# One chunk of a conv-attention block taken slot by slot on TensorE, VectorE's conv steps moved one place up, and fc1 as 32x32 tiles

## The reference, cut to what matters

```python
# layer 0
h = biasfree_ln(x, ln1_w)
x1 = gelu(depthwise3x3(h[:, :16]))            # local branch
q, k, v, lfeat = split(gelu(conv1x1(h[:, 16:])))   # 8 channels each
attn = swapaxes(softmax(avg_pool(q) @ max_pool(k).T, axis=1))
out = concat([x1, lfeat, attn @ v]) + x
m = biasfree_ln(out, ln2_w)
m = gelu(fc1(m))                              # 32 -> 128 channels
m = m + gelu(depthwise3x3(m) + pos_b)
X = out + fc2(m)                              # 128 -> 32 channels
# layer 1, over 256 pixels of every image
q, k, v = X.T @ Wq + bq, X.T @ Wk + bk, X.T @ Wv + bv
a = softmax(q @ k.T, axis=1)                  # 256 x 256, over the queries
y = X + (a @ v).T
```

## Time and profile before

| | us |
|---|---|
| median of three runs (lowest, highest) | 119.53 (118.51, 121.95) |
| the profiled execution's own time | 119.45 |
| its span, first to last instruction | 117.7 |
| TensorE matmul busy (share of the span) | 101.3 (86%) |
| ScalarE busy | 86.7 (74%) |
| VectorE busy | 75.2 (64%) |
| TensorE in the chain that ended last | 64% |

### The profile page before, as it was taken

How to read it: one execution, slowest core, us unless ns; L and a number is a source line. 1 busy time by engine, 2 the same in 40 slices (tenths; PEclk the granted TensorE clock), 3 DMA queues, 4 the chain that set the end, 5 groups by cost and what they waited for, 6 DMA issues and landing times.

```text
span 117.7 us, 5736 instructions
## 1 busy us (share of the span) xinstructions
PE 101.3 (86%) x2632; PEld 58.4 (50%) x2632; DVE 75.2 (64%) x152; ACT 86.7 (74%) x204; POOL 12.1 (10%) x22
## 2 busy tenths in 40 slices
PE   0394999789999899998999799999799999997660
PEld 0042677566684446832445464534364566575330
DVE  0007992133332989799957698964746579789851
ACT  4069991851785883889567989947889989898960
POOL 5010000000000000000000000598000040002300
PEclk9999999995589999999999999999999999999999
DMA  2880000000000000000000000000000020002022
GB/s 61 277 336 16 0 6 6 0 6 0 6 6 6 8 0 6 8 6 0 6 0 6 0 6 6 0 0 6 6 6 0 0 95 0 6 15 77 0 89 89
DMA packets 1751, 3.42 MB, mean 29 GB/s; under 512 B 320, under 2 KB 576, under 8 KB 1728
## 3 DMA queue, kind: packets, MB, share of 16 engines
q1 hardware_dynamic: 1584, 3.03, 7.4%
q10 hardware_dynamic: 144, 0.03, 0.2%
HBM read 2.01 MB, written 1.05 MB: 26 GB/s over the span
## 4 chain that ended last, share of the span: by engine, by line
PE 64%; ACT 16%; DVE 11%; DMA 3%; issue 3%; ACTq 0%; DVEq 0%
PE ps L372 13%; PE ps L295 10%; ACT prob L749 6%; PE ps L455 6%; PE ps L420 4%; PE ps L483 4%; ACT hpad L700 4%; DVE unit L917 3%; DMA first<-first_in 3%; PE ps L284 3%; PE ps L262 3%; PE ps L467 3%; PE ps L448 3%; ACT prob L736 3%; PE ps L307 2%
## 5 line engine op out<-in xcount | busy, mean ns | idle before, releaser
L372 PE MATMUL ps<-hpad,third 32*32 32x450 f32 (+2 forms) x864 | 36.5, 563 | 0.6 <-ACT hpad L700 0.5
L749 ACT ACTIVATE prob<-ps,smax 128x256 f32<-128x256 f32 x56 | 25.7, 479 | 3.7 <-DVE smax L964 3.7
L917 DVE SCALAR_TENSOR_TENSOR unit<-hpad,third,unit 128x544 f32<-128x544 f32 x32 | 23.8, 796 | 0.0
L964 DVE TENSOR_REDUCE smax<-ps 128x2 f32<-128x512 f32 x26 | 16.5, 683 | 6.5 <-PE ps L467 3.4
L372 PEld LDWEIGHTS ps<-hpad,third 32*32 32x32 f32 x864 | 14.0, 103 | 8.9 <-issue 4.2
L295 PE MATMUL ps<-npad,second 32*32 32x225 f32 (+2 forms) x576 | 14.6, 390 | 0.3 <-DVE npad L841 0.3
L239 POOL TENSOR_TENSOR v_tok<-v_tok,row_inv 128x256 f32<-128x256 f32 x7 | 5.1, 738 | 94.0 <-DVE row_inv L974 94.0
L700 ACT ACTIVATE hpad<-ps,third 128x1024 f32<-128x1024 f32 x8 | 8.7, 1116 | 4.5 <-PE ps L356 2.4
L749 ACT ACTIVATION_READ_ACCUMULATOR prob<-ps,smax 128x1 f32 x56 | 11.8, 211 | 0.0
L295 PEld LDWEIGHTS ps<-npad,second 32*32 32x32 f32 x576 | 9.2, 107 | 3.4 <-issue 1.7
L483 PE MATMUL ps<-prob,v_tok 128*32 128x256 f32 x128 | 8.1, 382 | 2.3 <-ACT prob L736 1.1
(11 more groups left out here) (83 smaller groups left out, 140.4 us busy)
## 6 DMA issues: line engine op xcount, KB each, us to landing
x<-x_in SPq DMA_DIRECT2D x4, 256.0 KB, 5.2
y<-m SPq DMA_DIRECT2D x3, 256.0 KB, 2.5
third<-third_in SPq DMA_DIRECT2D x1, 456.5 KB, 6.5
second<-second_in SPq DMA_DIRECT2D x1, 453.5 KB, 5.4
y<-m SPq DMA_DIRECT2D x2, 128.0 KB, 1.9
first<-first_in ACTq DMA_DIRECT2D x1, 33.0 KB, 4.1
```

What stands on the lines that cost most here:

```text
L372: last = pe.matmul(inside(pixels(ps[quadrant(rotated(r, g)), banks[g], :]), tap), c3("taps")[quadrant(r), tap * C:(tap + 1) * C], inside(p ...
L749: last = act.activation(prob[:, G * (slot_turn(s) % PROBS) + g, jt * NPIX:(jt + 1) * NPIX], ps[:, banks[q], jt * NPIX:(jt + 1) * NPIX], AC ...
L917: dve.scalar_tensor_tensor(out=sums, in0=source, scalar=weight, in1=sums, op0=ALU.mult, op1=ALU.add).then_inc(unit_step, 1)
L964: dve.tensor_reduce(smax[:, s, 2 * q:2 * q + 2], ps[:, banks[q], :].rearrange("p (j i) -> p j i", j=2), AX_X, ALU.max, negate=True).then_i ...
```

## The change

TensorE: fc1 of chunks 0 and 2 goes by `fc1_by_tiles`, and `fc1` is deleted. The taps of chunk 3's convolution are spread anew: before fc2 of chunk 2 stands tap 1 of groups 0 and 1 only, and its other half comes behind it. `queries_and_keys(2)` becomes a new `query_beside_key` for slot 4 (keys into bank 6, queries into bank 7, no tap in between) and for slot 5 (banks 4 and 5, half of tap 2 in between), each with its own semaphore step. Slot 4's scores go by halves as slot 5's did: quadrants 2 and 3 as soon as slot 4's key and query are biased, then quadrants 0 and 1, with tap 3 beside both. `scores_beside_tap` is only written in another way. Two taps, 7 and 8, are now left for the place behind `fc2_units(0, 6)`, where one was; `query_and_key(0, 4)` moves ahead of `weighted_values(2, 7)`.

ScalarE: only slot 4's key stays there; slot 5's key goes to VectorE.

VectorE: one more step of the chunk-0 convolution at each of three places, so that two steps fewer are left between the last maxima of slot 3 and X of slot 4; `query(4)`, `key(5)`, `query(5)`, and maxima of slot 4 by halves. Counts of semaphores follow.

```diff
@@ -163,7 +163,7 @@
             return {1: 1 + s % 2, 2: 3 + s % 2, 0: 5, 3: 6 + s % 2}[s // 2]
 
         def slot_of_qk(s):
-            return {0: 1, 1: 2, 6: 3, 7: 4}[s]
+            return {4: 1, 5: 2, 0: 3, 1: 4, 6: 5, 7: 6}[s]
 
         def slot_turn(s):
             return 2 * turn_of(s // 2) + s % 2
@@ -345,11 +345,6 @@
                                          start=True, stop=True)
                 last.then_inc(mixed, 1)
 
-            def fc1(k, g, bank):
-
-                pe.matmul(ps[:, bank, :], c3("fc1_w")[quadrant(g), :], m[quadrant(g), k, :],
-                          start=True, stop=True).then_inc(fc1_done, 1)
-
             def fc1_by_tiles(k, g, bank):
 
                 for c in range(G):
@@ -361,7 +356,7 @@
 
                 pe.wait_ge(normed[1], k + 1)
                 for g in range(G):
-                    fc1(k, g, banks[g])
+                    fc1_by_tiles(k, g, banks[g])
 
             def conv_taps(k, lo, hi, banks, groups=range(G), rows=range(G)):
 
@@ -438,6 +433,13 @@
                 project("wk", s, bank, 0)
                 project("wq", s, bank, 1).then_inc(qk_of_slot, 1)
 
+            def query_beside_key(s, key_bank, query_bank, tap, groups):
+
+                pe.wait_ge(X_ready, x_count(s))
+                project("wk", s, key_bank)
+                conv_taps(s // 2 + 1, tap, tap + 1, LOW, groups)
+                project("wq", s, query_bank).then_inc(qk_of_slot, 1)
+
             def values(k, bank):
 
                 pe.wait_ge(X_ready, x_count(2 * k + 1))
@@ -457,19 +459,21 @@
                                          slot(rstd, s)[quadrant(q), :], start=True, stop=True)
                 last.then_inc(scores_done, 1)
 
+            def scores_by_tiles(s, jt, quadrants, banks):
+
+                for q in quadrants:
+                    for c in range(G):
+                        at = jt * P + c * C
+                        last = pe.matmul(ps[quadrant(c), banks[q], jt * NPIX:(jt + 1) * NPIX],
+                                         slot(swapped, s)[quadrant(q), at:at + C],
+                                         slot(rstd, s)[quadrant(q), :], start=True, stop=True)
+                return last
+
             def scores_beside_tap(s, quadrants, banks, tap, conv_banks):
 
-                rows = [r for r in range(G) if r not in quadrants]
-                for jt in range(2):
-                    for q in quadrants:
-                        for c in range(G):
-                            at = jt * P + c * C
-                            last = pe.matmul(ps[quadrant(c), banks[q], jt * NPIX:(jt + 1) * NPIX],
-                                             slot(swapped, s)[quadrant(q), at:at + C],
-                                             slot(rstd, s)[quadrant(q), :], start=True, stop=True)
-                    if jt == 0:
-                        conv_taps(s // 2 + 1, tap, tap + 1, conv_banks, rows=rows)
-                last.then_inc(scores_done, 1)
+                scores_by_tiles(s, 0, quadrants, banks)
+                conv_taps(s // 2 + 1, tap, tap + 1, conv_banks, rows=[r for r in range(G) if r not in quadrants])
+                scores_by_tiles(s, 1, quadrants, banks).then_inc(scores_done, 1)
 
             def weighted_values(s, bank):
 
@@ -559,7 +563,7 @@
             pe.wait_ge(log_ready[1], 4)
             pe.wait_ge(normed[1], 3)
             for g in range(G):
-                fc1(2, g, HIGH[g])
+                fc1_by_tiles(2, g, HIGH[g])
             conv_taps(1, 7, 9, LOW)
 
             pe.wait_ge(hid_gelu, 6)
@@ -594,36 +598,40 @@
             conv_taps(3, 0, 1, LOW, (1, 2, 3))
             pe.wait_ge(v_ready, 1)
             conv_taps(3, 0, 1, LOW, (0,))
-            conv_taps(3, 1, 2, LOW)
+            conv_taps(3, 1, 2, LOW, (0, 1))
             pe.wait_ge(conv_gelu, 6)
             fc2_hidden_slots(2, (4, 5))
             fc2_conv_slots(2, (4, 5))
+            conv_taps(3, 1, 2, LOW, (2, 3))
+            query_beside_key(4, 6, 7, 2, ())
+            query_beside_key(5, 4, 5, 2, (2, 3))
+            pe.wait_ge(q_ready, 3)
+            pe.wait_ge(k_ready, 3)
+            scores_beside_tap(4, (2, 3), HIGH, 3, LOW)
             conv_taps(3, 2, 3, LOW, (0, 1))
-            queries_and_keys(2, (6, 7), (6, 7), 2, LOW, (2, 3))
-            conv_taps(3, 3, 4, LOW)
             pe.wait_ge(q_ready, 4)
-            pe.wait_ge(k_ready, 4)
-            scores(4, range(G), HIGH)
-            conv_taps(3, 4, 6, LOW)
+            pe.wait_ge(k_by_vector, 1)
+            scores_beside_tap(4, (0, 1), HIGH, 3, LOW)
+            conv_taps(3, 4, 5, LOW)
             pe.wait_ge(exp_done, 10)
             scores_beside_tap(5, (2, 3), HIGH, 6, LOW)
-            conv_taps(3, 7, 8, LOW)
+            conv_taps(3, 5, 6, LOW)
             pe.wait_ge(exp_done, 12)
             scores_beside_tap(5, (0, 1), HIGH, 6, LOW)
             pe.wait_ge(exp_done, 13)
             fc2_units(0, 6)
+            conv_taps(3, 7, 9, LOW)
+            pe.wait_ge(exp_done, 15)
+            query_and_key(0, 4)
             pe.wait_ge(exp_done, 14)
             weighted_values(2, 7)
-            conv_taps(3, 8, 9, LOW)
-            pe.wait_ge(exp_done, 15)
-            query_and_key(0, 4)
             pe.wait_ge(exp_done, 16)
             weighted_values(3, 5)
             pe.wait_ge(conv_gelu, 9)
             values(2, 0)
             pe.wait_ge(y_ready, 2)
             pe.wait_ge(q_ready, 5)
-            pe.wait_ge(k_by_vector, 1)
+            pe.wait_ge(k_by_vector, 2)
             scores(0, range(G), HIGH)
             pe.wait_ge(conv_gelu, 11)
             query_and_key(1, 2)
@@ -808,7 +816,7 @@
             conv_act(2, HIGH)
             unit_act(0)
             unit_act(2)
-            keys(2, (6, 7))
+            key_slot(4, 6)
             act.preload_act_table_set(exp_tables)
             pixel_exp(4, HIGH, (2, 3, 0, 1))
             pixel_exp(5, HIGH, (2, 3, 0, 1))
@@ -1011,26 +1019,30 @@
             conv_steps(14, 25)
             finish_block_slot(2, 2)
             finish_block_slot(3, 3)
-            conv_steps(25, 26)
+            conv_steps(25, 27)
             queries(1, (2, 3))
-            conv_steps(26, 27)
+            conv_steps(27, 28)
             maxima(2, range(G), LOW, 1)
-            conv_steps(27, 28)
+            conv_steps(28, 30)
             maxima(3, (0, 1), LOW, 2)
-            conv_steps(28, 29)
+            conv_steps(30, 31)
             maxima(3, (2, 3), LOW, 3)
-            conv_steps(29, 31)
+            conv_steps(31, 33)
             values(1, 0)
             invert_sums(2)
-            conv_steps(31, 34)
+            conv_steps(33, 36)
             invert_sums(3)
-            conv_steps(34, 36)
             finish_block_slot(4, 4)
             finish_block_slot(5, 5)
-            queries(2, (6, 7))
-            maxima(4, (2, 3, 0, 1), HIGH, 4)
-            maxima(5, (2, 3), HIGH, 5)
-            maxima(5, (0, 1), HIGH, 6)
+            dve.wait_ge(qk_of_slot, slot_of_qk(4))
+            query(4, 7, 0)
+            dve.wait_ge(qk_of_slot, slot_of_qk(5))
+            key(5, 4)
+            query(5, 5, 0)
+            maxima(4, (2, 3), HIGH, 4)
+            maxima(4, (0, 1), HIGH, 5)
+            maxima(5, (2, 3), HIGH, 6)
+            maxima(5, (0, 1), HIGH, 7)
             finish_block(0, 6)
             key_and_query(0, 4)
             finish(2, 7)
...
-            maxima(0, (0, 1), HIGH, 7)
-            dve.wait_ge(k_ready, 5)
+            maxima(0, (0, 1), HIGH, 8)
+            dve.wait_ge(k_ready, 4)
...
```

More of the change, by code:

```diff
@@ L635, in _ @@
             pe.wait_ge(q_ready, 6)
-            pe.wait_ge(k_ready, 5)
+            pe.wait_ge(k_ready, 4)
             for q in range(2):
@@ L646, in _ @@
             pe.wait_ge(q_ready, 8)
-            pe.wait_ge(k_ready, 7)
+            pe.wait_ge(k_ready, 6)
             scores(6, (0, 3), LOW)
@@ L1040, in _ @@
             invert_sums(5)
-            maxima(0, (0, 1), HIGH, 7)
-            dve.wait_ge(k_ready, 5)
+            maxima(0, (0, 1), HIGH, 8)
+            dve.wait_ge(k_ready, 4)
             query(1, 2)
             values(0, 1)
-            maxima(0, (2, 3), HIGH, 7)
+            maxima(0, (2, 3), HIGH, 8)
             finish_block_slot(6, 3)
             finish_block_slot(7, 0)
-            maxima(1, (0,), HIGH, 8)
-            maxima(1, (1,), HIGH, 9)
+            maxima(1, (0,), HIGH, 9)
+            maxima(1, (1,), HIGH, 10)
             dve.wait_ge(qk_of_slot, slot_of_qk(7))
             query(7, 0)
-            dve.wait_ge(k_ready, 6)
+            dve.wait_ge(k_ready, 5)
             query(6, 3)
-            maxima(1, (2, 3), HIGH, 10)
+            maxima(1, (2, 3), HIGH, 11)
             finish(4, 1)
             finish(5, 2)
-            maxima(6, (0, 3), LOW, 11)
-            maxima_of_two(6, 1, LOW, 12)
+            maxima(6, (0, 3), LOW, 12)
+            maxima_of_two(6, 1, LOW, 13)
             invert_sums(0)
             invert_sums(1)
-            maxima_of_two(7, 0, HIGH, 13)
```

(3 more changed lines are left out.)

## The result

The changed kernel takes 119.97 us (median of 20 runs, 118.69 to 122.41) where the kernel before takes 119.57 (20 runs, 117.65 to 123.07). The ratio of the comparable runs is 1.0094, interval 1.0051 to 1.0137: the change makes the kernel 0.9% slower, some 1.1 us, where 118.4 us, 1.1 us faster, was forecast. 119.97 lies in the range given, but the sign is wrong. Ratios compare fast executions with fast ones; slow are those over 1.5% above the fastest of their kernel.

A forecast was written before the change was run, and what follows sets the result against it. The middle was taken as bound by latency, a round of three engines, and what follows by TensorE. From 119.45 us, fc1 by tiles took 0.35 and the round, less the further tap, 0.70: 118.4 us, range 116.9 to 120.4.

The forecast's parts named there:

- fc1 by tiles at chunk 0: Chunk 0's fc1 as 32x32 records on TensorE: hidden gelu 0.2 us earlier, bounds -0.1 and +0.5.
- a gelu before 36.64: Sign in the changed kernel's timeline: ScalarE's first hidden gelu starts before 36.64 us.
- fc1 by tiles at chunk 2: Chunk 2's fc1 as 32x32 records on TensorE: 0.3 us gained, bounds -0.1 and +0.5.
- The round: Chunk 2's reordered work for slots 4 and 5: 1.90 us gained at slot 4's first exponential, 0.70 left at the end.
- First exponential: Slot 4's first exponential on ScalarE: at 80.92 instead of 82.82 us, 1.90 earlier, bounds 1.3 to 2.3.
- fc2 of the units: TensorE's fc2 behind slot 4's scores: moves from 88.23 to 86.33 us, as much earlier as the first exponential.
- further tap: Postponed tap ahead of slot 1's projections on TensorE: costs 1.20 us, bounds 0.8 to 1.3.
- ScalarE's wait ahead of slot 1's key: Sign: ScalarE idle for 1.3 to 1.5 us ahead of slot 1's key, at about 95.3, released by TensorE.
- VectorE's steps: Conv steps of 0.70 us moved earlier: the one ahead of slot 2's and 3's queries fills idle time, costing nothing.
- A: Rival, chance 0.20: the further tap behind the round is free, the full 1.90 us gets through; 117.2 us.
- C: Rival, chance 0.18: slot 4's scores held up, first exponential only 1.2 us earlier, the tap eats it; 119.1 us.
- B: Rival, chance 0.12: in TensorE's queue, 77 to 83 us, matmuls keep strict order, each record 38 ns; 1.0 slower, 120.5 us.

The follow-up runs named there:

- Chunk 0 wide: Changed kernel with chunk 0's fc1 wide again, chunk 2's still by tiles; 118.65 us, ratio 0.9899.
- yardstick: The "before again" profile, with which profiles at the full clock are compared; 119.0 us, span 117.2.
- third look: Kernel before, unchanged, profiled once more; 120.37 us, with a half-clock stretch again.
- + 16 records: Kernel before plus eight useless 8-column matmuls (16 records) while TensorE waits for the third chunk of x; 121.43 us, ratio 1.0253.
- round only: Changed kernel with fc1 of both chunks 0 and 2 wide again, as before; 119.08 us, ratio 0.998.
- Before + 96: Kernel before plus 48 useless matmuls (96 records) at the very start, while TensorE waits for its inputs; 118.78 us, ratio 0.983.
- changed + 128: Changed kernel plus 64 useless matmuls (128 records) at the very start, while TensorE waits for its inputs; 118.53 us, ratio 1.0002.
- before again: Kernel before, unchanged, profiled again with the full clock throughout; 119.0 us, span 117.2.
- changed + 96: Changed kernel plus 48 useless matmuls (96 records) at the very start, while TensorE waits for its inputs; 117.42 us, ratio 0.9787.

## Why the prediction was wrong

**fc1 by tiles at chunk 0: the step that failed.** I took 0.2 us gained, with bounds of -0.1 and +0.5. Measured: 1.27 lost in the changed kernel (2.61 to 3.88), and nothing to speak of with the edges elsewhere: 2.57, 0.04 gained, its 32 loads within 0.35 and no break. All the working of that step prices records by tiles, drains and columns; it has no term for where TensorE's instructions come from, though the page of before shows 20 packets of them. The bounds were both drawn from rows in which the block was there in time. My sign for it, a gelu before 36.64, was also badly chosen: the gelu came at 35.93, since the attention half was quicker in that execution, and only the time from the mark shows the loss.

**fc1 by tiles at chunk 2: right in sign, half in size.** 0.3 was forecast. "Chunk 0 wide" shows 0.28 against the yardstick (27.66 to 27.38), but that is the yardstick's own pauses. Of the five other profiles with both fc1 wide, four (before, its third look, + 16 records, round only) have 27.30 to 27.32 and one, with 96 records, 28.89; the kernel with only this edit has 27.16, 0.16 less, and the one with both fc1 by tiles 27.35, with other pauses. The 0.16 is one profile's. Its timing doesn't bear even that out, as told. In the changed kernel the stage is 27.86, though "changed + 128", with the same work and nearly the same edges, has 27.31; what makes that half microsecond between two executions I did not settle. So without any break the two fc1 terms would have been worth some 0.2 (0.04 and 0.16), not the 0.35 carried.

**The round: right, then cut by pauses.** Times behind slot 2's first exponential (us):

| | before again | changed | chunk 0 wide | changed + 96 |
|---|---|---|---|---|
| value projection of chunk 1 | 7.34 | 7.75 | 7.34 | 7.34 |
| X of slot 4 | 13.49 | 13.00 | 12.59 | 12.60 |
| key of slot 4 | 15.81 | 14.68 | 14.27 | 14.28 |
| first exponential of slot 4 | 18.88 | 17.41 | 17.00 | 17.01 |
| fc2 of the units | 24.29 | 22.82 | 22.64 | 22.42 |
| key of slot 1 | 32.43 | 31.97 | 31.78 | 31.57 |
| last exponential | 49.01 | 48.56 | 48.37 | 48.14 |

First exponential 1.90 earlier forecast; 1.88 measured in "chunk 0 wide", and 1.47 in the changed kernel, which is 0.41 late from the value projection on and stays some 0.4 behind changed + 96 through every row. That is ahead of the round, in a tap of chunk 3 that all kernels have, and it is an edge too: counted from slot 2's first exponential, the two traces agree load for load within 0.05 us up to the 1896th, and the 1897th, 11 blocks behind the 484th, comes 0.39 late (timeline of PEld, changed kernel):

```profile
69.61 1.19 PEld L367 LDWEIGHTS ps<-hpad,third 32*32 32x32 f32 x40 [0.29 <-issue]
```

fc2 of the units: 1.90 forecast, 1.65 and 1.47 measured. Behind it 1.20 was to go to the further tap, leaving 0.70 at slot 1's key and at the end: 0.65 and 0.64 in "chunk 0 wide", 0.46 and 0.45 in the changed kernel, 0.86 and 0.87 in changed + 96. ScalarE's wait ahead of slot 1's key, forecast at 1.3 to 1.5, is 1.34. VectorE's steps cost nothing, as forecast.

**The sum.** Its bounds were too narrow for its own terms: fc1 0 to 0.6, the first exponential 1.3 to 2.3 and the tap 0.8 to 1.3 give 117.35 to 119.45, not 117.7 to 119.3. The result lies above both, because the fc1 term is outside its bounds.

**The rivals.** A (the further tap is free) is refuted: TensorE 8.20 of 8.20 and the wait of 1.34. C (the round doesn't do what it says) is refuted by X and the first exponential. B was right that TensorE's queue would be where the time is lost and right in size (1.0 slower, by accident), but wrong in mechanism and place: matmuls of other tiles did overlap in the round, a record didn't cost 38 ns, and the loss lay 40 us earlier, in fc1. The largest loss had no rival of its own.

**What stays open.** What triggers a fetch is inferred from starts 0.5 to 1.9 us behind the last edge; the runs don't exclude another trigger. How much of the gain with 96 records belongs to the attention half isn't separated: before again and changed do the same work ahead of the mark with the same edges, and their two executions still differ there by 1.2 us, so one profile each does not settle 1 us. "Before + 96" shows it: its three stages are together 1.5 us longer than before again's, its span (117.0) about equal, and its timing 1.7% faster.

## What to carry to other kernels

Before tiling a matmul finer on TensorE, count weight loads and matmuls: where the rows of the weight loads show "issue" at a fixed distance in records (here 128.5), apart from the pauses at changes of shape, and the page has a queue of kind "instruction", more records have a second price, which depends on where a block's edge falls. Put the edges where TensorE waits or drains anyway, and put dense records of short matmuls not right behind an edge; useless matmuls in idle time at the start move the whole grid, and two or three such shifts should be timed before any edit of the order is judged. An edit that changes the count ahead of a dense stretch is judged with the shift that suits it, not with the old one.

## What the runs showed of the hardware that I had not expected

TensorE's instructions arrive in packets of 16 KB that take about 1.0 us. From a pause at an edge TensorE went on 1.2 us (changed, 34.77) and 1.3 us (16 records more, 36.12) behind the packet's end, and from passing one edge to passing the next it took 3.46 us (31.31 to 34.77, changed) and 4.27 (31.85 to 36.12). Over 128.5 records that is 27 to 33 ns a record, where attention's taps start one every 15 ns (63 loads in 0.94 us). Before again passed the same two edges within 3.19 us (32.45 to 35.64), and what it paused for there was the change of shape behind the wide fc1.

Sixteen records in idle time cost the kernel before 3.0 us, and 96 gained the changed kernel 2.4 us. An edit of nothing moved this kernel by more than the change did.

The Trainium skill (Advanced Engine Details and Errata, ISA Cache) gives a cache with lines of 16 KB, 256 instructions, and only two of them. A fetch that starts only once the edge before has been passed agrees with two lines, one in use and one being filled; its larger size for TensorE in the same list would let TensorE run on, and the 1.25 us pauses speak against that here.
